# Softmax over the neighbours moved from one pass over all batches into the neighbour sum, batch by batch

## The reference, cut to what matters

```python
h = lrelu(_bn(feat @ W1.T, g1, b1))
h = lrelu(_bn(h @ W2.T, g2, b2))
h = lrelu(_bn(h @ W3.T, g3, b3))
att = jax.nn.softmax(h[..., 0], axis=-1)
xk = x.transpose(0, 2, 1)[bidx, idx]
agg = jnp.einsum('bnkc,bnk->bnc', xk, att)
return x + agg.transpose(0, 2, 1)
```

## Time and profile before

| | |
|---|---|
| median of 3 runs | 6893.18 us (6890.46 to 6906.41) |
| the profiled execution's own time | 6878.53 us |
| its span, first to last instruction | 6876.1 us |
| mean granted TensorE clock | 0.894 |
| busy: TensorE, VectorE, ScalarE, GpSimd | 5928.1, 6084.7, 4455.0, 4813.1 us |
| softmax over all batches | 5584.3 to 5633.3 us of the span |
| from there to the first one-hot product | to 5664.9 us |
| neighbour sum, first product to the end | 1211.2 us, 32 batches |

### The profile page before, as it was taken

The page is one execution under the profiler, slowest core; times in us unless marked ns, Lnnn a source line. Parts: engine busy times, 40 slices in busy tenths (PEclk is TensorE's granted clock), DMA queues, the critical chain, the costliest instruction groups (busy, mean ns, idle before and its releaser), DMA issues. The chain is left out here.

```text
span 6876.1 us, 226732 instructions
## 1 busy us (share of the span) xinstructions
PE 5928.1 (86%) x84308; PEld 3577.8 (52%) x84308; DVE 6084.7 (88%) x8460; ACT 4455.0 (65%) x17112; POOL 4813.1 (70%) x4750
## 2 busy tenths in 40 slices
PE   8888888888888888888888888888857949999999
PEld 4555555545454555455545555555532327767776
DVE  7999999999999999999999999999976578777876
ACT  6777777777777777777777777777741543333333
POOL 6788888888888888888888888888870013333332
PEclk9988988889888888888888888889868979999999
DMA  1222222222222222222222222222223003332322
GB/s 34 75 71 84 80 78 71 78 71 78 71 87 80 78 72 83 80 77 71 77 71 77 72 75 92 73 76 83 70 95 72 0 22 85 84 92 80 91 80 76
DMA packets 245853, 508.79 MB, mean 74 GB/s; under 512 B 155868, under 2 KB 169436, under 8 KB 210780
## 3 DMA queue, kind: packets, MB, share of 16 engines
q1 hardware_dynamic: 244700, 493.37, 22.7%
HBM read 377.93 MB, written 65.01 MB: 64 GB/s over the span
## 5 line engine op out<-in xcount | busy, mean ns | idle before, releaser
L653 ACT ACTIVATE prob<-SC,row_max 128x64 f32<-128x64 f32 x6144 | 1830.1, 325 | 1080.2 <-DVE row_max L998 1037.2
L769 POOL TENSOR_TENSOR k_bd<-k_t,head_mask 128x512 f32<-128x512 f32 x1536 | 1700.6, 1128 | 7.4 <-POOL dist_row L747 4.5
L653 ACT ACTIVATION_READ_ACCUMULATOR prob<-SC,row_max 128x1 f32 x6144 | 1336.8, 218 | 0.0
L982 DVE FIND_INDEX8 nbr<-top,dist 128x8 uint16<-128x1024 f32 x1024 | 1234.5, 1217 | 0.0
L978 DVE MAX8 top<-dist 128x8 f32<-128x1024 f32 x1024 | 1192.8, 1205 | 12.2 <-DVE y_b L1021 9.9
L780 POOL TENSOR_TENSOR prob<-prob,row_rec 128x512 f32<-128x512 f32 x768 | 813.0, 1059 | 544.0 <-DVE row_rec L1006 543.3
L553 PE MATMUL SC<-k_bd,q_t 128*64 128x256 f32 x6144 | 923.8, 426 | 0.0
L980 DVE MATCH_REPLACE8 dist<-top,dist 128x1024 f32<-128x1024 f32 x768 | 923.4, 1206 | 0.0
L561 PE MATMUL PT<-ident,prob 128*128 128x128 f32 x3072 | 543.7, 304 | 401.5 <-ACT prob_t L660 396.2
L1780 DVE TENSOR_TENSOR d_oh_a<-lo,iota_a 128x4096 bf16<-128x4096 bf16 x256 | 583.8, 2291 | 245.8 <-PE DM L1632 245.6
L1673 ACT ACTIVATE dense<-DM 128x512 f32<-128x512 f32 x512 | 305.4, 597 | 756.5 <-PE DM L1632 756.2
(11 more groups left out here) (201 smaller groups left out, 10825.7 us busy)
## 6 DMA issues: line engine op xcount, KB each, us to landing
low_all<-low_scratch SPq DMA_DIRECT2D x256, 1024.0 KB, 5.1
placed<-compact SPq DMA_DIRECT2D x256, 192.0 KB, 3.8
ctx<-in_ctx SPq DMA_DIRECT2D x32, 512.0 KB, 4.1
mask<-in_mask SPq DMA_DIRECT2D x32, 512.0 KB, 7.3
xb<-in_x SPq DMA_DIRECT2D x32, 512.0 KB, 4.8
x_scratch<-xb SPq DMA_DIRECT2D x32, 512.0 KB, 5.0
y_scratch<-y_b SPq DMA_DIRECT2D x32, 512.0 KB, 6.6
d_x<-x_scratch SPq DMA_DIRECT2D x32, 512.0 KB, 5.0
```

The lines of the kernel that those rows point to most:

```text
L653: last = act.activation(prob[:, s % 4, g * CHUNK:(g + 1) * CHUNK], SC[:, s % 2, g * CHUNK:(g + 1) * CHUNK], ACT.Exp, bias=row_max[:, s % 2 ...
L769: last = pool.tensor_tensor(k_bd[:, q % KEY_BUFS, ch, :].rearrange("p (h k) -> p h k", h=8), kk, hm, ALU.mult)
L982: last = dve.max_index(nbr[:, uu % BPB, t, k * 8:(k + 1) * 8], best, row)
```

## The change

The softmax leaves `batch_norms`. What stays there is that GpSimd copies the raw values of the third layer to `att` by rows, two neighbours at a time, as VectorE transposes them; `gain3` and `shift3` outlive the block. In `neighbour_sum` ScalarE applies gain and shift in the copy to `at_n` that it made already. VectorE then does leaky ReLU, maximum and subtraction of the next batch after tile 3 (`exponents`), with the one-hot blocks behind it; ScalarE the exponential after half-tile 8 (`powers`); VectorE sum, reciprocal, product and transpose after tile 4 (`weights`, which waits for the exponential). `moments_of` moves from tile 4 to tile 5, `normalise` from half-tile 13 to 15. Ahead of the first batch both engines now clear `placed` after the weights, and VectorE waits for the constants only ahead of the one-hot blocks. TensorE's and SP's programs are as before. `att` shrinks from 32 to 30 columns a row.

```diff
@@ -1297,6 +1291,12 @@
                 pool.tensor_scalar(var_eps[0:rows, 0:width], var[0:rows, 0:width], 1.0, EPS, ALU.mult, ALU.add).then_inc(plink, 1)
                 pool.wait_ge(plink, n + 2)
                 mark(pool.tensor_tensor(inv[0:rows, 0:width], var_eps[0:rows, 0:width], minus_half[0:rows, 0:width], ALU.pow))
+                if n == 1:
+                    by_row = att[:, :, :].rearrange("p (b t) k -> p b t k", t=NT)
+                    for m in range(PAIRS_K):
+                        pool.wait_ge(z3_turned, m + 1)
+                        pool.tensor_copy(by_row[:, :, :, 2 * m:2 * m + 2], S[:, 0, 2 * m:2 * m + 2, :].rearrange("p k (t b) -> p b t k", t=NT)).then_inc(laid_out, 1)
+            pool.wait_ge(laid_out, PAIRS_K)
...
-            wait(act, "gain3")
-            act.wait_ge(z3_turned, PAIRS_K)
-            by_row = S[:, 0, :, :].rearrange("p k (t b) -> p b t k", t=NT)
-            for x in range(PARTS_S):
-                mine = att[:, x * SHARE:(x + 1) * SHARE, 0:K].rearrange("p (b t) k -> p b t k", t=NT)
-                share = SHARE // NT
-                act.activation(mine, by_row[:, x * share:(x + 1) * share], ACT.Identity, scale=gain[2][:, 0:1],
-                               bias=shift[2][:, 0:1]).then_inc(u3_ready, 1)
-            for x in range(PARTS_S):
-                mine = att[:, x * SHARE:(x + 1) * SHARE, 0:K]
-                act.wait_ge(lowered, x + 1)
-                act.activation(mine, mine, ACT.Exp).then_inc(powered, 1)
...
             norm(3, st3, 128, 1, given["g3"], given["b3"])
-            wide = [128, SHARE, K]
-            dve.memset(att[:, :, K:KP], 0.0)
-            for x in range(PARTS_S):
-                own = slice(x * SHARE, (x + 1) * SHARE)
-                dve.wait_ge(u3_ready, x + 1)
-                link(dve.scalar_tensor_tensor(att[:, own, 0:K], att[:, own, 0:K], SLOPE, att[:, own, 0:K], ALU.mult, ALU.max))
-                link(dve.tensor_reduce(top[:, own], att[:, own, 0:K], AX.X, ALU.max))
-                dve.tensor_tensor(att[:, own, 0:K], att[:, own, 0:K], top[:, own].unsqueeze(2).to_broadcast(wide), ALU.subtract).then_inc(lowered, 1)
-            for x in range(PARTS_S):
-                own = slice(x * SHARE, (x + 1) * SHARE)
-                dve.wait_ge(powered, x + 1)
-                link(dve.tensor_reduce(total[:, own], att[:, own, 0:K], AX.X, ALU.add))
-                link(dve.reciprocal(total[:, own], total[:, own]))
-                dve.tensor_tensor(att[:, own, 0:K], att[:, own, 0:K], total[:, own].unsqueeze(2).to_broadcast(wide), ALU.mult)
+            wait(dve, "gain3")
...
@@ -1650,8 +1633,14 @@
 
 
                 act.wait_ge(at_ready, START + b(1))
-                act.activation(at_n[:, :].rearrange("p (n k) -> p n k", k=KP), keep["att"][:, bass.ds(b(NT), NT), :],
-                               ACT.Identity).then_inc(copied_in, 1)
+                act.activation(at_n[:, :, 0:K], keep["att"][:, bass.ds(b(NT), NT), :], ACT.Identity, scale=keep["gain3"][:, 0:1],
+                               bias=keep["shift3"][:, 0:1]).then_inc(copied_in, 1)
+
+            def powers(b):
+
+
+                act.wait_ge(lowered, START + b(1, 1))
+                act.activation(at_n[:, :, 0:K], at_n[:, :, 0:K], ACT.Exp).then_inc(powered, 1)
...
@@ -1673,10 +1662,13 @@
                     act.activation(dst, src, ACT.Identity).then_inc(dense_copied, 1)
                     if x == 1 and not is_last(i, u):
                         weights(counter(i, u + 1))
-                    if x == 13 and not is_first(i, u):
+                    if x == 8 and not is_last(i, u):
+                        powers(counter(i, u + 1))
+                    if x == 15 and not is_first(i, u):
                         normalise(counter(i, u - 1), (u - 1) % BPD)
 
             weights(counter(0, 0))
+            powers(counter(0, 0))
...
             pool.wait_ge(consts_in, START + 16 * len(CONSTS))
+            split_weights(counter(0, 0), 0, False)
             pool.memset(placed[:, 1, :, :, :, :], 0.0).then_inc(cleared[1], 1)
-            split_weights(counter(0, 0), 0, False)
             all_batches(pool, body)
...
         @block.vector
         def _(dve):
-            dve.wait_ge(consts_in, START + 16 * len(CONSTS))
...
+            def exponents(b):
+
+
+                own, wide = at_n[:, :, 0:K], [128, NT, K]
+                dve.wait_ge(copied_in, START + b(1, 1))
+                dve.scalar_tensor_tensor(own, own, SLOPE, own, ALU.mult, ALU.max).then_inc(leaky, 1)
+                dve.wait_ge(leaky, START + b(1, 1))
+                dve.tensor_reduce(top[:, :], own, AX.X, ALU.max).then_inc(highest, 1)
+                dve.wait_ge(highest, START + b(1, 1))
+                dve.tensor_tensor(own, own, top[:, :].unsqueeze(2).to_broadcast(wide), ALU.subtract).then_inc(lowered, 1)
+
             def weights(b):
-                dve.wait_ge(copied_in, START + b(1, 1))
+                own, wide = at_n[:, :, 0:K], [128, NT, K]
+                dve.wait_ge(powered, START + b(1, 1))
+                dve.tensor_reduce(total[:, :], own, AX.X, ALU.add).then_inc(scaled, 1)
+                dve.wait_ge(scaled, START + b(3, 1))
+                dve.reciprocal(scale[:, :], total[:, :]).then_inc(scaled, 1)
+                dve.wait_ge(scaled, START + b(3, 2))
+                dve.tensor_tensor(own, own, scale[:, :].unsqueeze(2).to_broadcast(wide), ALU.mult).then_inc(scaled, 1)
+                dve.wait_ge(scaled, START + b(3, 3))
                 dve.wait_ge(at3_ready, START + b(1))
-                dve.transpose(at_t[:, :], at_n[:, :]).then_inc(at_ready, 1)
+                dve.transpose(at_t[:, :], at_n[:, :, :].rearrange("p t k -> p (t k)")).then_inc(at_ready, 1)
...
@@ -1833,18 +1842,22 @@
                     if t == 2 and not is_last(i, u):
                         indices(counter(i, u + 1), (u + 1) % BPD)
                     if t == 3 and not is_last(i, u):
+                        exponents(counter(i, u + 1))
+                        one_hot_blocks(counter(i, u + 1))
+                    if t == 4 and not is_last(i, u):
                         weights(counter(i, u + 1))
-                    if t == 4 and not is_first(i, u):
+                    if t == 5 and not is_first(i, u):
                         moments_of(counter(i, u - 1), (u - 1) % BPD)
-                    if t == 5 and not is_last(i, u):
-                        one_hot_blocks(counter(i, u + 1))
                     if t >= 6 and not is_last(i, u):
                         compact_blocks(counter(i, u + 1), i, (u + 1) % BPD, t - 6)
 
+            dve.memset(at_n[:, :, K:KP], 0.0)
+            indices(counter(0, 0), 0)
+            exponents(counter(0, 0))
+            dve.wait_ge(consts_in, START + 16 * len(CONSTS))
+            one_hot_blocks(counter(0, 0))
+            weights(counter(0, 0))
             dve.memset(placed[:, 0, :, :, :, :], 0.0).then_inc(cleared[0], 1)
-            indices(counter(0, 0), 0)
-            weights(counter(0, 0))
-            one_hot_blocks(counter(0, 0))
             for h in range(2):
                 compact_blocks(counter(0, 0), 0, 0, h)
...
         attention_and_neighbours(nc, dram, keep)
-        keep["att"] = es.enter_context(nc.sbuf_tensor("att_all", [128, N * NT, KP], F32))
+        keep["att"] = es.enter_context(nc.sbuf_tensor("att_all", [128, N * NT, K], F32))
+        for name in ("gain3", "shift3"):
+            keep[name] = es.enter_context(nc.sbuf_tensor(name, [128, 1], F32))
```

More of the change, by code:

```diff
@@ L1106 @@
 LOADS = (0, 4, 12, 20, K)
-PARTS_S = 4
-SHARE = N * NT // PARTS_S
 BN_ROW = (("W1", 36), ("W2", 18), ("W3", 3), ("g1", 6), ("g2", 3), ("g3", 1), ("b1", 6), ("b2", 3), ("b3", 1))
@@ L1163, in batch_norms @@
         inv = sb("inv", [128, 2])
-        gain = [sb(f"gain{n}", [128, w]) for n, w in ((1, 2), (2, 1), (3, 1))]
-        shift = [sb(f"shift{n}", [128, w]) for n, w in ((1, 2), (2, 1), (3, 1))]
-        top = sb("top", [128, N * NT])
-        total = sb("total", [128, N * NT])
+        gain = [sb(f"gain{n}", [128, w]) for n, w in ((1, 2), (2, 1))] + [keep["gain3"]]
+        shift = [sb(f"shift{n}", [128, w]) for n, w in ((1, 2), (2, 1))] + [keep["shift3"]]
         Z = ps("Z", [128, BANKS, 512])
@@ L1188, in batch_norms @@
         u2_ready = sem("u2_ready")
-        u3_ready = sem("u3_ready")
-        lowered = sem("lowered")
-        powered = sem("powered")
+        laid_out = sem("laid_out")
         block = es.enter_context(nc.Block())
@@ L1473, in neighbour_sum @@
         iota_m = sb("iota_m", [128, 8], BF16)
-        at_n = sb("at_n", [128, NT * KP])
+        at_n = sb("at_n", [128, NT, KP])
+        top = sb("top", [128, NT])
+        total = sb("total", [128, NT])
+        scale = sb("scale", [128, NT])
         at_t = sb("at_t", [128, NT * KP])
@@ L1500, in neighbour_sum @@
         at_ready = sem("d_at_ready")
+        leaky = sem("leaky")
+        highest = sem("highest")
+        lowered = sem("lowered")
+        powered = sem("powered")
```

(1 more changed line is left out.)

## The result

The changed kernel takes 7028.25 us (median of 4 runs, 7021.45 to 7035.27), the kernel before 6893.77 us beside it: ratio 1.0192 [1.0174, 1.0209], 1.9% slower. The prediction was 7000 us in a range of 6948 to 7036. The profiled execution's span is 7018.6 us, its own time 7021.45, its mean granted clock 0.880.

A forecast was written before the change was run, and what follows sets the result against it. The softmax was taken as serial and the neighbour sum as bound by TensorE. Softmax -49.0, start -11.0 and neighbour sum with clock +167 gave +107 on 6893.2: 7000 us, range 6948 to 7036.

The forecast's parts named there:

- the likeliest case: Whole kernel: TensorE rests in 30 of 32 batches with a lower clock behind, +107 us to 7000; chance 0.55.
- The softmax: Serial softmax stretch over all batches, with TensorE idle, is removed in full: -49.0 us.
- Ahead of the first batch: From the work before to the first product: 20.7 us instead of 31.7, -11.0; table load not waiting for the maximum, 1.3 more.
- `compact` beside GpSimd's clearing: Ahead of the first batch: GpSimd's clearing doesn't hold VectorE's `compact`, 0 us; 9 us if held; dear copies or clearing, chance 0.08.
- GpSimd's copies in the third layer: Fifteen copies beside VectorE's leaky ReLU cost 0 us, nearest to the cast; 18.5 if dear; dear copies or clearing, chance 0.08.
- TensorE's rest: After tile 4, TensorE waits for VectorE's late read of `AG`: 4.2 us in 30 of 32 batches.
- First batch: In the first batch, whose products VectorE paces, the wait for the exponential adds about 5.5 us.
- Waits for `placed`: TensorE's waits for `placed` inside loop passes go, since TensorE comes later: -9.5 us.
- The 0.5 us at the next tile 0: `oh_a` for the next tile 0 comes 0.5 us late at 17 boundaries; vanishes if the clock slows TensorE.
- E: The time at which TensorE ends tile 4 and wants to start the first half's sum.
- The clock: Behind each of TensorE's 30 rests, a lower clock costs 1.5 us; rival without a fall of the clock 6964, chance 0.28.
- The rival that the exponential is at hand: After tile 4, VectorE doesn't wait for the exponential, TensorE rests 1.7 us: -13, 6880 us; chance 0.04.

The follow-up runs named there:

- two ways around the read: Changed kernel with VectorE's read of `AG` ahead of the weights, or with TensorE's guard asking only for the half it overwrites: 6968.64 and 6968.80 us.
- exponential at 6: Changed kernel with ScalarE's exponential behind half-tile 6 instead of 8 (the earlier exponential): 6902.68 us, ratio to the kernel before 1.0017.
- early order: Changed kernel with `exponents` after tile 2, exponential behind half-tile 3, `weights` after tile 3, read at tile 4, `normalise` at half-tile 13: 6823.46 us.
- early, read late: The early order with only the read of `AG` put back from tile 4 to tile 5: 6848.42 us, ratio to the kernel before 0.9924.
- the fill of four: Changed kernel with four extra large matmuls, their result unused, on TensorE in its wait ahead of the first half's sum: 6961.85 us.
- read first: Changed kernel with VectorE reading `AG` and taking the moments after tile 4, ahead of the next batch's weights: 6968.64 us, ratio to before 1.0108.
- guard by half: Changed kernel with TensorE's guard ahead of the first half's sum asking only for the read of that half: 6968.80 us, ratio to before 1.0111.
- the experiment: Changed kernel with both halves of `placed` cleared ahead of the first weights again, as in the kernel before: 7031.22 us, ratio to before 1.0207.

## Why the prediction was right, point by point

The direction, the range and the likeliest case held; the sum was 28 us short (+107 against +134.5). The path and the rest were right, in place and in length. The price of the clock behind it was too low by 30 us, which is the whole shortfall: the smaller errors (2.3 us ahead of the first batch, 2.6 in the rests, 6.7 at the loop boundaries, for which the sum had nothing, the other way) cancel nearly, and that is luck.

- **The softmax:** -49.0, and -49.0 measured: nothing of it stays; SyncE's first DMA comes half a microsecond behind the norm's last instruction.
- **Ahead of the first batch:** -11.0 forecast, -8.7 measured. The table load didn't wait for the maximum, which gave the 1.3 us named in the prediction, but VectorE's transposes waited 2.37 us with `POOLq` named as releaser, which no row of before had shown; the transposed weights end at 8.8 us instead of 7.4. VectorE's clearing then began 1.24 us later still, and `compact` began at its end, 2.2 us after GpSimd's split. The prediction had the split done at 11.5 and the clearing at 12.6; they were done at 12.9 and 15.2.
- **`compact` beside GpSimd's clearing:** 0 forecast with 9 as far end; it is 0. Six instructions take 3.63 us in the midst of a clearing of 10.34. By that row the rule of the Trainium skill (SBUF — State Buffer, "Who interferes with whom") holds for this pair.
- **GpSimd's copies in the third layer:** 0, and +0.2 measured (65.0 us from norm to norm, 64.8 before). GpSimd's timeline there:

```profile
5569.85 3.09 POOL L1298 COPY att_all<-sph_rows 128x512 f32<-128x512 f32 x1 [0.33 <-DVE sph_rows L1414]
...
5586.27 1.03 POOL L1298 COPY att_all<-sph_rows 128x512 f32<-128x512 f32 x1 [2.40 <-DVE sph_rows L1414]
```

A copy takes 1.03 us by itself (the estimate by the Trainium skill, GPSIMD Engine Reference, "Performance pitfalls for Q7 kernels", was 1.24, too long), but 11 of the 15 run beside VectorE's leaky ReLU and last 3.1. VectorE isn't held by them: its leaky ReLUs still come every 3.43 us. The answer was right, its reason half so: the copies didn't fit into the gap, GpSimd was the one that waited. The 0 itself was chosen for being nearest to the cast's row, and that the wait would fall on GpSimd, where nobody was late for it, was luck.
- **TensorE's rest:** the heart of the forecast. 4.2 us in 30 batches, 126 in all; measured 128.6 in 31 waits (the last of them 0.5). VectorE's wait for the exponential: 2.6, measured 2.54 in the batch shown. Behind it the granted clock is 0.5, as the prediction's list of signs has it. The two ways around the read, the earlier exponential and the early order each moved the rest as the chain says.
- **First batch:** +5.5, measured +5.6 (36.3 us between its first product and the second's, 30.7 before).
- **Waits for `placed`:** -9.5, and they are gone.
- **The 0.5 us at the next tile 0:** taken as vanishing with a slower TensorE, and it did; TensorE waits for no one-hot matrix in the change behind the first batch. The chain written out for it held for its first half: the split ends at E + 9.4 (forecast 9.5), the first half of `compact` at E + 11.5 (11.4). Then GpSimd's addition fell on the one-hot matrix of tile 7 (3.82 us instead of 2.29) and not on the second half of `compact`, which ends at E + 18.3 (17.9) all the same. The 0.5 was for a TensorE that had rested 4.2 us; once it doesn't rest, the same lateness shows as waits of 1.46 and 1.83 us in the batch shown, of which the second stays away where a loop boundary follows.
- **The clock:** this is the term that was mis-sized. 1.5 us a rest, 45 in all; the large matmuls lost 75.2 us, 2.5 for each of the 30. The prediction had 2.1 as what 4.2 us at half speed lose and took a value between that and the transposes' 0.9, without a reason. The 0.9 was what the eight transposes alone lost, in 1.96 us; the low level went on behind them. The eight matmuls behind a rest of 4.2 to 4.3 us take 5.6 to 6.7 us, 6.13 in the mean, and so bear its whole price: a loss of 2.45 us is an estimated 4.9 us at half speed, where 4.2 were worked out from the earlier trace rows behind the loop boundaries. Its own 2.1 would have brought the sum to +125.

With the measured sizes: 5.6 + 128.6 + 75.2 - 9.5, less 6.7 by which the waits at the loop boundaries are shorter (57.1 before, 50.4 after), is 193.2, against the stage's +194.0.

The rival that the exponential is at hand (6880) was made an experiment: it gave 6902.68, 14 us above the kernel before beside it. The rest was 1.6 us, as that rival had it; it gave such a rest no price of the clock, and behind 15 of 30 it had one.

## What to carry to other kernels

When work is moved into an engine's idle time, ask where in that engine's order it waits, and what stands behind it there: 2.2 us of new work a batch fitted well into VectorE's idle time, and 2.5 us of waiting for one exponential of 0.4 us made a loss of 134 us out of one of 14, because the read that releases TensorE's accumulator stood behind it. A rest of TensorE can cost more than its length, here 2.5 us of lower clock on 4.2 of rest, so a producer should be asked for its result a whole step before the consumer comes, as in the early order, which turned 1.9% slower into 0.9% faster with the same instructions. And taking one wait away can uncover another that it had hidden: both direct repairs got back less than half.

## What the runs showed of the hardware

How much TensorE loses behind a rest, by the eight large matmuls that follow (3.68 us at full clock), over all such rests (in the change and with the exponential at 6 the last batch's, 0.5 us long and followed by 3.67, is left out):

| rest before them | rests | eight matmuls take |
|---|---|---|
| 0.52 to 0.57 us (early, read late) | 29 | 3.67 or 3.70 in all |
| 0.15 to 0.79 us, behind the fill of four | 30 | 3.67 or 3.70 in all |
| 1.3 to 1.8 us (exponential at 6) | 30 | 3.67 or 3.70 in 15, 5.1 to 6.8 in 15 |
| 4.2 to 4.3 us (after) | 30 | 5.56 to 6.66, mean 6.13 |

- At 4.2 us every rest is followed by the lower level, at 0.6 none, at 1.6 half, and there the length of the rest doesn't tell which: 1.60 was followed by 3.70 and by 5.40. The two batches of a loop pass always share the outcome (14 passes). With two waits of 1.5 and 1.8 us close together (read first, guard by half) it showed again. What decides between them is open.
- The table load for the exponential began at 5592.08, 4.5 us before the subtraction for which the exponential waits had ended (5596.56): it isn't held by the instruction's own wait.
- A copy of 256 16-bit elements a partition on VectorE, 0.22 us by itself, took 4.04 beside GpSimd's clearing and 7.38 in the experiment, each time to its end, while `compact` on the same engine ran beside the same clearing at 0.6 us a piece. The Trainium skill (SBUF — State Buffer, "Who interferes with whom") tells the two kinds apart: a copy can run in a mode that takes the port pair shared with GpSimd and is then blocked as long as GpSimd holds it, a product of two inputs meets only GpSimd's reads. These rows agree with it; no run here varied the copy's form.
